# An attention and FFN block on one core: the probabilities of fifteen tiles transposed in 32x32 blocks on VectorE and put together through DRAM

## Chip, cores and metric

One Trainium2 chip, one of its cores. The metric is the device time of one execution of the whole program in microseconds. Three runs of the kernel before are known; their median is the number that the change is compared with. The profile comes from one further execution.

## What is computed

x has the shape 32 x 256 x 256 (batch, tokens, features), the context 32 x 77 x 256. One layer of cross-attention with a residual, then one gated FFN with a residual, all in fp32:

```
x = x + attention(layernorm(x), ctx)      8 heads of 32, 77 keys, causal mask, biases on q, k, v and out
h = silu(y @ w1.T * s1) * (y @ w2.T * s2)       y = layernorm(x), 256 -> 1024
h = gelu(h @ h1.T * h1s)                        1024 -> 1024
h = gelu(h @ h2.T * h2s)                        1024 -> 1024
x = x + h @ w3.T * s3                           1024 -> 256
attention:  p = softmax(mask(q @ k.T / sqrt(32)));  out = (p @ v) @ Wo.T + bo
```

The weights of the FFN are ternary, which one piece of a split fp32 number keeps exactly. So each of the FFN's products is made of two fast products (type fp32r), with the high and the low part of the activations. The attention's products are plain fp32.

## The kernel before

**Tiles and staging.** The 8192 tokens are 16 tiles of 512, each two batch entries (n = 0 and 1) of 256 tokens. All weights stay in SBUF. A prologue (FIRST, one_pass with f = None) does the attention of tile 0, computes the keys and values of all later tiles and spills them to DRAM. Then a loop runs whose pass f does the FFN of tile f, the attention of tile f + 1 and the load and first layernorm of tile f + 2. Two passes behind the loop finish the last tiles. So the attention of tile 0 is in the prologue and that of fifteen tiles in passes.

**The order.** ORDER (lines 57 to 66) is one list of steps written by hand. Each engine goes through it and issues what it has to do for each step; the engines meet through semaphores only. A step of the FFN is L1 n, L2 n, L3 n (n = 0 to 7, sixteen products of 128x512 for L2 and L3, eight for L1) or L4 n. The attention's steps stand between them: S (scores), MASK, MAX, SUB, EXP, SOFT (sum, reciprocal, product: the probabilities are finished), PT (transposes), PV (probabilities by values), O (output projection), LN2S and LN2A (second layernorm), T2 (its transpose), LN1S, ROWS, LN1A (first layernorm of the tile after), Q, and CTX (loads for the next tile). The attention uses four PSUM banks (ab), the FFN four others (fb).

**The steps that the change touches.** SOFT n leaves the probabilities of batch entry n in probs[:, 2n:2n+2, :], tokens on the partitions, for each token 8 heads of 77 keys (lines 906 to 912). The product with the values wants keys on the partitions. For that TensorE transposes in PT 0 to 3 (lines 598 to 613), one step for each 128 tokens, eight transposes each (L611), two steps for an entry; ScalarE copies four heads of a step from PSUM (L766) and VectorE the other four (L918) into attn_t for entry 0 and attn_t2 for entry 1, [77 keys, 8 heads, 256 tokens]. attn_t lies where L1's operand ln2_hi lies, attn_t2 where xln and out_sb lie, so the second copy waits until the output of the tile before is stored. PV n (lines 614 to 624) multiplies them with v_sb, both entries in a row; PV 0 waits for all copies. ScalarE copies the result to heads_t (L773), which O reads.

**Queues.** All transfers are issued by SyncE, in the order of the list: in CTX the keys (L361), the values (L362), and, when x1 is finished, x_in (L323) and ln_t (L326) of the tile after; in LN1S and ROWS two small transfers through DRAM (L331, L336); in L4 the output (L417). SyncE waits for each step's semaphore before it comes to the next.

**VectorE** also takes the low parts of the FFN's activations: L849 and L854 in L1, L860 in L2 and L3. TensorE needs those of L2 only at L3 0. A step of L2 n from 4 on needs ScalarE's evictions of step n - 4.

ln1_t, which holds the transposed x of the tile after, is used up to Q of the tile; k_t, the keys, up to S 1:

```
ln1_t, _ = put("ln1_t", [P, KD, TILE])
...
k_t, _ = put("k_t", [P, HG, NB * TK])
```

Of the kernel before, what the change touches and what calls it, by code (L numbers as in the profile page):

```python
# [16 lines left out]
F32 = mybir.dt.float32  # L17
# [6 lines left out]
P = 128  # L24
B, TQ, TK, D = 32, 256, 77, 256
H = 8
# [16 lines left out]
def column_of(head):  # L43
# [13 lines left out]
ORDER = [  # L57
    ("L1", 0), ("S", 0), ("MASK", 0), ("L1", 1), ("L1", 2), ("MAX", 0), ("S", 1), ("L1", 3), ("SUB", 0),
    ("L1", 4), ("L1", 5), ("L1", 6), ("L1", 7), ("L1E", 0),
    ("EXP", 0), ("MASK", 1), ("MAX", 1), ("SUB", 1), ("EXP", 1), ("SOFT", 0), ("L2", 0), ("SOFT", 1), ("L2", 1),  # L60
# [5 lines left out]
]  # L66
# [40 lines left out]
def build_kernel(nc, x, x_t, ctx_t, ctx_later, w_att, vectors, w1, w2, h1, h2, w3, out):  # L107
# [4 lines left out]
    with ExitStack() as es:  # L112
# [59 lines left out]
        out_sb, out_at = put("out_sb", [P, NQ, D])  # L172
        assert out_at == xln_at + 4 * NQ * D
        attn_t2, _ = put("attn_t2", [TK, H, TQ], at=xln_at)
        ln1_t, _ = put("ln1_t", [P, KD, TILE])
        x1_keep, _ = put("x1_keep", [P, NQ, D])
        ln1_rows, _ = put("ln1_rows", [P, 2, TILE], at=out_at)

        k_t, _ = put("k_t", [P, HG, NB * TK])
        v_sb, v_at = put("v_sb", [TK, NB, D])  # L180
        ctx_sb, _ = put("ctx_sb", [P, KD, NB * TK], at=v_at)


# [27 lines left out]
        flag, _ = put("flag", [1, 1], I32)  # L211

        rows_dram = nc.dram_tensor("ln1_rows_dram", (2, TILE), F32, kind="Internal").ap()
        k_dram = nc.dram_tensor("k_later_dram", (P, HG, LATER), F32, kind="Internal").ap()
        v_dram = nc.dram_tensor("v_later_dram", (LATER, D), F32, kind="Internal").ap()
        k_dram_tiles = k_dram.rearrange("p m (t c) -> t p m c", c=NB * TK)
# [36 lines left out]
        s_copied = sem("s_copied")  # L253
        sum_done, rsum_done, probs_ready = sem("sum_done"), sem("rsum_done"), sem("probs_ready")
        pt_ready, pt_act_done, pt_dve_done = sem("pt_ready"), sem("pt_act_done"), sem("pt_dve_done")
        pv_ready, heads_done, o_ready = sem("pv_ready"), sem("heads_done"), sem("o_ready")
        x_biased, x1_done, x1_kept = sem("x_biased"), sem("x1_done"), sem("x1_kept")
        t2_ready, ln2hi_done, ln2t_done = sem("t2_ready"), sem("ln2hi_done"), sem("ln2t_done")
# [62 lines left out]
        def _(sp):  # L321
# [51 lines left out]
            def one_pass(f, a, b, general):  # L373
                for step, n, t in steps(f, a, b):
                    if step in FFN and general:
                        for i, src in enumerate(general_chunks(step, n)):
                            c = chunk_base[step, n] + i
                            sp.wait_ge(ring_used, CHUNKS * f + c + 1)
                            sp.dma_start(ring[c % 2][:], src).then_inc(ring_loaded[c % 2], 16)
                    if step == "KEEP":  # L380
                        if n == 0:
                            for c in range(NP):
                                sp.wait_ge(piece_loaded[c], 16)
                        for c in KEPT[n]:
                            keep_piece(c)
                    if step == "SPILL" and n == 0:
                        sp.wait_ge(kx_done, 4)
                        spill_keys((0, 1), k_spilled[0])
                    if step == "SPILL" and n == 1:
                        sp.wait_ge(kx_done, 2 * NG - 1)  # L390
                        spill_keys(range(2, NG), k_spilled[1])
                        sp.wait_ge(vx_done, 5)
                        spill_values(range(0, 10))
                        sp.wait_ge(vx_done, (NCH + 1) // 2)
                        spill_values(range(10, NCH))
                    if step == "CTX":
                        sp.wait_ge(pv_ready, NB * t)
                        if f is None:
                            load_ctx(t)
                        else:  # L400
                            sp.wait_ge(k_spilled[0], 32)
                            sp.wait_ge(k_spilled[1], 16 * (NG - 2))
                            sp.wait_ge(v_spilled, 48)
                            load_keys_values(t, f)
                            sp.wait_ge(x1_done, t)
                            load_x(t)
                            load_xt(t)
                    if step == "LN1S" and f is not None:
                        write_rows(t)
                    if step == "ROWS":  # L410
                        sp.wait_ge(stored, 32 * f + 32)
                        load_rows(t)
                    if step == "L4":
                        half = slice(2 * n, 2 * n + 2)
                        sp.wait_ge(out_ready, 2 * f + n + 3)
                        dst = out_tiles[f] if isinstance(f, int) else out_tiles[bass.ds(f, 1)].rearrange("a p j d -> (a p) j d")
                        sp.dma_start(dst[:, half, :], out_sb[:, half, :]).then_inc(stored, 16)  # L417
# [29 lines left out]
        def _(pe):  # L447
# [35 lines left out]
            def one_pass(f, a, b, general):  # L483
                for step, n, t in steps(f, a, b):
# [113 lines left out]
                    if step == "PT":  # L598
                        if n % 2 == 0:
                            pe.wait_ge(probs_ready, NB * t + n // 2 + 1)  # L600
                        if n == 0:
                            pe.wait_ge(s_copied, NB * t + NB)
                            pe.wait_ge(masked, NB * t + NB)
                        if n == 1 and f is None:
                            pe.wait_ge(ln1t_done, 2)
                        if n == 2:
                            pe.wait_ge(pt_act_done, NQ * t + 2)
                            pe.wait_ge(pt_dve_done, NQ * t + 2)
                        pair = (2, 0, 2, 0)[n]
                        for h in range(H):  # L610
                            mm = nc.tensor.transpose(ab[0:TK, pair + h // 4, (h % 4) * P:(h % 4 + 1) * P],  # L611
                                                     probs[:, n, column_of(h) * TK:(column_of(h) + 1) * TK], id32[:])
                        mm.then_inc(pt_ready, 1)
                    if step == "PV":
                        if n == 0:
                            pe.wait_ge(pt_act_done, NQ * t + NQ)
                            pe.wait_ge(pt_dve_done, NQ * t + NQ)
                        bank = (2, 0)[n]
                        for g in range(HG):
                            for h in range(4):  # L620
                                mm = nc.tensor.matmul(ab[HD * h:HD * (h + 1), bank, g * TQ:(g + 1) * TQ],  # L621
                                                      v_sb[:, n, (4 * g + h) * HD:(4 * g + h + 1) * HD],
                                                      (attn_t, attn_t2)[n][:, 4 * g + h, :], start=True, stop=True)
                        mm.then_inc(pv_ready, 1)
                    if step == "O":
                        pe.wait_ge(heads_done, NB * t + NB)
# [61 lines left out]
        def _(act):  # L688
            def one_pass(f, a, b):
                for step, n, t in steps(f, a, b):  # L690
# [69 lines left out]
                    if step == "PT":  # L760
                        act.wait_ge(pt_ready, NQ * t + n + 1)
                        q0 = (n % 2) * P
                        pair = (2, 0, 2, 0)[n]
                        if n == 2 and f is not None:
                            act.wait_ge(stored, 32 * f + 32)
                        nc.scalar.copy((attn_t, attn_t2)[n // 2][:, 0:4, q0:q0 + P],  # L766
                                       ab[0:TK, pair, :].rearrange("p (h q) -> p h q", h=4)).then_inc(pt_act_done, 1)
                        if f is None and n < 2:
                            nc.scalar.copy(attn_t[:, 4:8, q0:q0 + P],
                                           ab[0:TK, pair + 1, :].rearrange("p (h q) -> p h q", h=4)).then_inc(pt_dve_done, 1)  # L770
                    if step == "PV":
# [14 lines left out]
        def _(dve):  # L786
# [42 lines left out]
            def one_pass(f, a, b):  # L829
                for step, n, t in steps(f, a, b):  # L830
# [75 lines left out]
                    if step == "SOFT":  # L906
# [3 lines left out]
                        nc.vector.reciprocal(per_head(rtotal, n), per_head(total, n)).then_inc(rsum_done, 1)  # L910
                        dve.wait_ge(rsum_done, NB * t + n + 1)
                        nc.vector.tensor_tensor(heads_of(n), heads_of(n), over_keys(rtotal, n), ALU.mult).then_inc(probs_ready, 1)
                    if step == "PT" and (f is not None or n >= 2):
                        dve.wait_ge(pt_ready, NQ * t + n + 1)
                        q0 = (n % 2) * P
                        if n == 2 and f is not None:
                            dve.wait_ge(stored, 32 * f + 32)
                        nc.vector.tensor_copy((attn_t, attn_t2)[n // 2][:, 4:8, q0:q0 + P],  # L918
                                              ab[0:TK, (2, 0, 2, 0)[n] + 1, :].rearrange("p (h q) -> p h q", h=4))\
                            .then_inc(pt_dve_done, 1)  # L920
# [144 lines left out]
```

## Time and profile before

| | |
|---|---|
| runs | 1598.69 us median of 3 (1598.31 to 1598.72) |
| profiled execution | 1598.01 us |
| its span, first to last instruction | 1596.2 us |
| granted TensorE clock, mean | 0.999 |
| TensorE busy | 1585.9 us, 8902 products |
| VectorE, ScalarE, GpSimd busy | 791.3, 728.5, 123.0 us |
| DMA | 67.73 MB, mean 42 GB/s |

The span leaves out what lies before the first and behind the last instruction, 1.8 us. Products on TensorE are pipelined: one begins before the last one ends, so the distance between the starts of two is what one costs in a row, and the duration of one is longer than that. In a timeline equal instructions that follow each other are merged into one row with their count; its second column is the time from the first one's start to the last one's end.

### The profile page before, as it was taken

The numbers are of one execution on the slowest core, as the hardware profiler recorded it, in microseconds if no ns is written. First come the engines' busy times: TensorE is split into PE (matmuls) and PEld (weight loads), VectorE is DVE, ScalarE is ACT, GpSimd is POOL, SyncE is SP. The second block draws the span as 40 slices with busy tenths as digits, with TensorE's granted clock in tenths as the row PEclk, the third lists the DMA queues.
The fourth block names the chain that finished last, engine by engine and source line by source line (L and its number), as shares of the span: only waits on it lengthen the run. The fifth ranks groups of instructions, "written<-read, shape, count | busy, mean of one in ns | idle before, by whom it ended". The sixth has DMA issues, their size and how long they took to land.

```text
span 1596.2 us, 22214 instructions
## 1 busy us (share of the span) xinstructions
PE 1585.9 (99%) x8902; PEld 1299.4 (81%) x8902; DVE 791.3 (50%) x1246; ACT 728.5 (46%) x1073; POOL 123.0 (8%) x134
## 2 busy tenths in 40 slices
PE   9999999999999999999999999999999999999998
PEld 6788888888888888888888888888888888888887
DVE  6653735447363464634537354464634537354332
ACT  4653534436353453534436354453634536354342
POOL 1001010010100101001010100101001010100000
PEclk9999999999999999999999999999999999999999
DMA  9921010100101001010000101001010010100000
GB/s 381 349 95 41 13 34 26 34 20 7 47 13 34 26 8 40 13 34 26 22 28 10 47 13 34 26 8 40 13 34 26 8 40 13 37 24 1 14 1 14
DMA packets 29349, 67.73 MB, mean 42 GB/s; under 512 B 6326, under 2 KB 14734, under 8 KB 26510
## 3 DMA queue, kind: packets, MB, share of 16 engines
q1 hardware_dynamic: 29326, 67.41, 11.8%
q8 instruction: 16, 0.26, 0.1%
q14 instruction: 7, 0.06, 0.0%
HBM read 43.00 MB, written 12.86 MB: 35 GB/s over the span
## 4 chain that ended last, share of the span: by engine, by line
PE 97%; DMA 1%; SPq 1%; DVE 0%; ACT 0%; issue 0%; ACTq 0%
PE ffn_banks L455 81%; PE att_banks L631 3%; PE att_banks L611 3%; PE att_banks L578 3%; PE att_banks L595 2%; PE att_banks L621 2%; DMA h_bits<-in_h 1%; PE att_banks L641 1%; SPq L365 0%; PE ffn_banks L664 0%; ACT junk L696 0%; SPq L344 0%; PE ffn_banks L656 0%; DVE inexact L834 0%; PE att_banks L566 0%
## 5 line engine op out<-in xcount | busy, mean ns | idle before, releaser
L455 PE MATMUL ffn_banks<-a_hi,h_sb 128*128 128x512 f32 x1024 | 405.8, 396 | 0.0
L455 PE MATMUL ffn_banks<-b_hi,h_sb 128*128 128x512 f32 x1024 | 399.7, 390 | 0.0
L455 PE MATMUL ffn_banks<-a_lo,h_sb 128*128 128x512 f32 x1024 | 399.0, 390 | 0.0
L455 PE MATMUL ffn_banks<-b_lo,h_sb 128*128 128x512 f32 x1024 | 398.5, 389 | 0.0
L860 DVE TENSOR_TENSOR b_lo<-b_f,b_hi 128x512 fp32r<-128x512 f32 x128 | 87.2, 691 | 288.2 <-ACT b_hi L731 288.2
L455 PEld LDWEIGHTS ffn_banks<-a_hi,h_sb 128*128 128x128 f32 x1024 | 192.3, 188 | 44.7 <-issue 6.2
L730 ACT ACTIVATE a_f<-ffn_banks,vec 128x512 f32<-128x512 f32 x128 | 88.3, 690 | 301.7 <-PE ffn_banks L455 301.7
L455 PEld LDWEIGHTS ffn_banks<-b_lo,h_sb 128*128 128x128 f32 x1024 | 192.3, 188 | 39.4
L455 PEld LDWEIGHTS ffn_banks<-b_hi,h_sb 128*128 128x128 f32 x1024 | 192.3, 188 | 39.4
L455 PEld LDWEIGHTS ffn_banks<-a_lo,h_sb 128*128 128x128 f32 x1024 | 192.4, 188 | 38.5
L860 DVE TENSOR_TENSOR a_lo<-a_f,a_hi 128x512 fp32r<-128x512 f32 x128 | 94.6, 739 | 258.4 <-ACT a_hi L731 258.4
L730 ACT ACTIVATE b_f<-ffn_banks,vec 128x512 f32<-128x512 f32 x128 | 88.1, 689 | 280.1 <-PE ffn_banks L455 278.7
L455 PE MATMUL ffn_banks<-ln_hi,w_sb 128*128 128x512 f32 x512 | 203.5, 398 | 0.6 <-DVE v_later L888 0.6
L455 PE MATMUL ffn_banks<-ln_lo,w_sb 128*128 128x512 f32 x512 | 200.4, 391 | 0.0
L714 ACT ACTIVATE a_f<-ffn_banks,vec 128x512 f32<-128x512 f32 x128 | 88.3, 690 | 163.1 <-PE ffn_banks L455 163.1
L455 PE MATMUL ffn_banks<-w_sb,a_hi 128*128 128x256 f32 x512 | 129.3, 294 | 0.8 <-DVE a_lo L860 0.8
L455 PE MATMUL ffn_banks<-w_sb,a_lo 128*128 128x256 f32 x512 | 123.6, 283 | 0.0
L849 DVE SCALAR_TENSOR_TENSOR a_f<-ffn_banks,vec,a_f 128x512 f32<-128x512 f32 x128 | 95.9, 749 | 52.9 <-PE ffn_banks L455 51.6
L455 PEld LDWEIGHTS ffn_banks<-ln_hi,w_sb 128*128 128x128 f32 x512 | 96.1, 188 | 22.7 <-issue 1.0
L455 PEld LDWEIGHTS ffn_banks<-ln_lo,w_sb 128*128 128x128 f32 x512 | 96.2, 188 | 19.4
L455 PEld LDWEIGHTS ffn_banks<-w_sb,a_hi 128*128 128x128 f32 x512 | 98.2, 192 | 4.7 <-issue 3.3
L455 PEld LDWEIGHTS ffn_banks<-w_sb,a_lo 128*128 128x128 f32 x512 | 98.2, 192 | 3.4 <-issue 3.3
(101 smaller groups left out, 1713.7 us busy)
## 6 DMA issues: line engine op xcount, KB each, us to landing
h_bits<-in_h SPq DMA_DIRECT2D x8, 1024.0 KB, 19.2
h_sb<-h_bits SPq DMA_DIRECT2D x8, 1024.0 KB, 8.4
out<-out_sb SPq DMA_DIRECT2D x32, 256.0 KB, 2.0
x_in<-in_x SPq DMA_DIRECT2D x15, 512.0 KB, 3.6
ln_t<-in_x_t SPq DMA_DIRECT2D x14, 512.0 KB, 4.3
ln_rows<-ln_rows_dram SPq DMA_DIRECT2D x14, 512.0 KB, 3.8
w_bits<-in_w SPq DMA_DIRECT2D x3, 1024.0 KB, 12.1
w_sb<-w_bits SPq DMA_DIRECT2D x3, 1024.0 KB, 6.6
```

The source lines that it names most:

```text
L455: mm = nc.tensor.matmul(psum, left, right, start=(k == 0 and part == 0), stop=(k == rows - 1 and part == 1))
L578: mm = nc.tensor.matmul(ab[:, m, :], wq_sb[:, k, m * P:(m + 1) * P], ln1_t[:, k, :], start=(k == 0), stop=(k == KD - 1))
L595: mm = nc.tensor.matmul(ab[:, h, at:at + TK], q_t[rows, g, tokens], k_t[rows, g, n * TK:(n + 1) * TK], start=True, stop=True)
L611: mm = nc.tensor.transpose(ab[0:TK, pair + h // 4, (h % 4) * P:(h % 4 + 1) * P], probs[:, n, column_of(h) * TK:(column_of(h) + 1) * TK], i ...
L621: mm = nc.tensor.matmul(ab[HD * h:HD * (h + 1), bank, g * TQ:(g + 1) * TQ], v_sb[:, n, (4 * g + h) * HD:(4 * g + h + 1) * HD], (attn_t, at ...
L631: mm = nc.tensor.matmul(ab[:, 2 + j // 2, (j % 2) * D:(j % 2 + 1) * D], heads_t[:, k, j * P:(j + 1) * P], wo_sb[:, k, :], start=(k == 0), ...
L641: mm = nc.tensor.transpose(ab[:, k, j * P:(j + 1) * P], xln[:, j, k * P:(k + 1) * P], id32[:])
L714: nc.scalar.activation(a_f32[:, n, :], fb[:, 2 * (n % 2), :], ACT.Silu, scale=s1_sb[:, n:n + 1]).then_inc(silu_done, 1)
L730: nc.scalar.activation(f32[:, n, :], fb[:, n % 4, :], ACT.Gelu, scale=scale[:, n:n + 1])
L849: nc.vector.scalar_tensor_tensor(out=a_f32[:, n, :], in0=fb[:, 2 * (n % 2) + 1, :], scalar=s2_sb[:, n:n + 1], in1=a_f32[:, n, :], op0=ALU. ...
L860: nc.vector.tensor_tensor(lo[:, n, :], f32[:, n, :], hi[:, n, :].bitcast(F32), ALU.subtract).then_inc(done, 1)
```

## The change

Only the tiles of the passes are changed; the prologue keeps PT. Each entry n has two new steps. DT n on VectorE: three block transposes of probs, each 32x32 block by itself, so that in the result keys lie on 32 partitions and tokens in runs of 32. Two take 32 keys of each of the 16 pairs of a head and a half of 128 tokens (blocks, 128 x 512 each), the third takes the last 16 keys (tail_blocks, 128 x 256). MV n on SyncE: stores blocks (512 KB) and tail_blocks (128 KB) to DRAM, waits for both, and issues four loads that put the four groups of 32 partitions side by side in attn_t or attn_t2: two of 32 partitions (256 KB each) and two of 13 partitions (52 KB each). PV n waits for the loads of its own entry and reads the tokens in runs of 32. blocks lies in ln1_t, tail_blocks in k_t; there is one of each, so DT 1 waits for the stores of MV 0. The list has PV behind L2 5 instead of L2 4, and O and CTX behind L2 7.

```diff
 ORDER = [
-    ("EXP", 0), ("MASK", 1), ("MAX", 1), ("SUB", 1), ("EXP", 1), ("SOFT", 0), ("L2", 0), ("SOFT", 1), ("L2", 1),
-    ("L2", 2), ("PT", 0), ("PT", 1), ("L2", 3), ("PT", 2), ("PT", 3), ("L2", 4), ("PV", 0), ("PV", 1),
-    ("L2", 5), ("L2", 6), ("O", 0), ("CTX", 0), ("L2", 7),
-    ("L3", 0), ("LN2S", 0), ("L3", 1), ("L3", 2), ("LN2A", 0), ("LN1S", 0), ("L3", 3), ("L3", 4), ("ROWS", 0),
+    ("EXP", 0), ("MASK", 1), ("MAX", 1), ("SUB", 1), ("EXP", 1), ("SOFT", 0), ("DT", 0), ("L2", 0), ("SOFT", 1), ("DT", 1),
+    ("L2", 1), ("MV", 0), ("L2", 2), ("MV", 1), ("L2", 3), ("L2", 4), ("L2", 5), ("PV", 0), ("PV", 1),
+    ("L2", 6), ("L2", 7), ("O", 0), ("CTX", 0), ("L3", 0), ("LN2S", 0), ("L3", 1), ("L3", 2), ("LN2A", 0), ("LN1S", 0), ("L3", 3), ("L3", 4), ("ROWS", 0),
...
+        blocks, _ = put("blocks", [P, 2, H * NB * 32], at=ln1_at)
+        tail_blocks, _ = put("tail_blocks", [P, H // 2 * NB * 32], at=k_at)
...
@@ SyncE
+                    if step == "MV":
+                        done = 2 * (NB * (t - 1) + n)
+                        sp.wait_ge(blocked, done + 1)
+                        sp.dma_start(blocks_dram[n], blocks[:]).then_inc(blocks_out, 16)
+                        sp.wait_ge(blocked, done + 2)
+                        sp.dma_start(tails_dram[n], tail_blocks[:]).then_inc(blocks_out, 16)
+                        if n == 0:
+                            sp.wait_ge(up_ready, KH * f + KH)
+                        else:
+                            sp.wait_ge(stored, 32 * f + 32)
+                        sp.wait_ge(blocks_out, 16 * done + 32)
+                        dst = (attn_t, attn_t2)[n][:].rearrange("k h q -> k (h q)").rearrange("k (r i) -> k r i", r=4)
+                        for c in range(2):
+                            src = blocks_dram[n][:, c, :].rearrange("(r k) i -> k r i", r=4)
+                            sp.dma_start(dst[32 * c:32 * c + 32], src).then_inc(blocks_back[n], 16)
+                        part = H * NB * 16
+                        for g in range(HG):
+                            src = tails_dram[n].rearrange("(r g k) i -> g k r i", r=4, g=HG)[g, 3:16]
+                            sp.dma_start(dst[64:TK, :, part * g:part * g + part], src).then_inc(blocks_back[n], 16)
@@ TensorE
                     if step == "PV":
-                        if n == 0:
-                            pe.wait_ge(pt_act_done, NQ * t + NQ)
-                            pe.wait_ge(pt_dve_done, NQ * t + NQ)
+                        if f is not None:
+                            pe.wait_ge(blocks_back[n], 64 * t)
+                        elif n == 0:
+                            pe.wait_ge(pt_act_done, NQ)
+                            pe.wait_ge(pt_dve_done, NQ)
                         bank = (2, 0)[n]
+                        by_block = (attn_t, attn_t2)[n][:].rearrange("k h q -> k (h q)")\
+                            .rearrange("k (r g j h q) -> k g h j r q", r=4, g=HG, j=NB, h=4)
                         for g in range(HG):
                             for h in range(4):
+                                probs_t = (attn_t, attn_t2)[n][:, 4 * g + h, :] if f is None else by_block[:, g, h]
@@ VectorE
+                    if step == "DT":
+                        dve.wait_ge(probs_ready, NB * t + n + 1)
+                        if n == 1:
+                            dve.wait_ge(blocks_out, 64 * t - 32)
+                        heads = probs[:, 2 * n:2 * n + 2, :].rearrange("p j (h g c) -> p g (j h) c", g=HG, c=TK)
+                        for c in range(2):
+                            op = nc.vector.transpose(blocks[:, c, :], heads[:, :, :, 32 * c:32 * c + 32])
+                        op.then_inc(blocked, 1)
+                        tails = probs[:, 2 * n:2 * n + 2, :].rearrange("p j (h c) -> p (j h) c", c=TK)[:, :, TK - 16:TK]
+                        nc.vector.transpose(tail_blocks[:], tails).then_inc(blocked, 1)
```

In the copies of PT on ScalarE and VectorE the conditions on f and the wait for `stored` fall away, since PT is left only in the prologue; `n == 1 and f is None` in TensorE's PT becomes `n == 1`.

## Rows read from the trace of the kernel before

**Rows 1.** The page, part 1: busy time, share of the span, instructions.
```profile
PE 1585.9 (99%) x8902; PEld 1299.4 (81%) x8902; DVE 791.3 (50%) x1246; ACT 728.5 (46%) x1073; POOL 123.0 (8%) x134
```

**Rows 2.** Busy times in one loop pass; last: granted clock, DMA share, GB/s.
```profile
738.26:834.57 96.31, 96.31 (x546) 79.17 (x545) 48.38 (x77) 44.00 (x65) 7.83 (x8) 1.00 0.08 25
```

**Rows 3.** The page, part 4: the chain that ended last, by engine and line.
```profile
PE ffn_banks L455 81%; PE att_banks L631 3%; PE att_banks L611 3%; PE att_banks L578 3%; PE att_banks L595 2%; PE att_banks L621 2%; DMA h_bits<-in_h 1%; PE att_banks L641 1%; SPq L365 0%; PE ffn_banks L664 0%; ACT junk L696 0%; SPq L344 0%; PE ffn_banks L656 0%; DVE inexact L834 0%; PE att_banks L566 0%
```

**Rows 4.** Waits of TensorE: in total, times, longest.
```profile
PE att_banks L611 <- DVE probs L912: 1.2, 1, 1.2
...
PE att_banks L621 <- DVE attn_t L918: 0.3, 1, 0.3
```

**Rows 5.** Timeline of TensorE, 757 to 800 us: start, length, instruction, count.
```profile
759.09 0.39 PE L455 MATMUL ffn_banks<-a_hi,h_sb 128*128 128x512 f32 x1
...
769.97 1.91 PE L611 MATMUL att_banks<-id,probs 128*77 128x128 f32 x16
771.63 0.48 PE L455 MATMUL ffn_banks<-a_hi,h_sb 128*128 128x512 f32 x1
...
775.36 1.91 PE L611 MATMUL att_banks<-id,probs 128*77 128x128 f32 x16
777.03 0.48 PE L455 MATMUL ffn_banks<-a_hi,h_sb 128*128 128x512 f32 x1
...
780.85 1.93 PE L621 MATMUL att_banks<-attn_t,v_sb 77*32 77x256 f32 x32
782.71 0.50 PE L455 MATMUL ffn_banks<-a_hi,h_sb 128*128 128x512 f32 x1
```

**Rows 6.** Groups of instructions by line and form: busy us, mean ns, idle before.
```profile
L611 PE MATMUL att_banks<-id,probs 128*77 128x128 f32 x512 | 61.1, 273 | 1.2 <-DVE probs L912 1.2
...
L918 DVE COPY attn_t<-att_banks 77x512 f32<-77x512 f32 x62 | 39.6, 679 | 0.0
...
L621 PE MATMUL att_banks<-attn_t,v_sb 77*32 77x256 f32 x512 | 30.9, 382 | 0.3 <-DVE attn_t L918 0.3
```

**Rows 7.** Timeline of VectorE in the same pass.
```profile
766.75 1.45 DVE L912 TENSOR_TENSOR probs<-probs,rtotal 128x1232 f32<-128x1232 f32 x1
768.96 0.69 DVE L860 TENSOR_TENSOR b_lo<-b_f,b_hi 128x512 fp32r<-128x512 f32 x1 [0.77 <-ACT b_hi L731]
769.57 1.43 DVE L908 TENSOR_REDUCE total<-probs 128x16 f32<-128x1232 f32 x1
...
771.32 1.44 DVE L912 TENSOR_TENSOR probs<-probs,rtotal 128x1232 f32<-128x1232 f32 x1
...
793.75 1.23 DVE L926 TENSOR_TENSOR x<-att_banks,x_in 128x1024 f32<-128x1024 f32 x1 [1.46 <-PE att_banks L631]
```

**Rows 8.** Timeline of SyncE's queue, 700 to 850 us: when it issued, for how long.
```profile
740.57 4.10 SPq L417 DMA_DIRECT2D out<-out_sb  x2
782.99 0.58 SPq L361 DMA_DIRECT2D k_t<-k_later_dram  x1
...
795.14 0.37 SPq L323 DMA_DIRECT2D x_in<-in_x  x1
795.60 0.38 SPq L326 DMA_DIRECT2D ln_t<-in_x_t  x1
```

**Rows 9.** DMA issues by transfer: count, size, median us from issue to landing.
```profile
out<-out_sb SPq DMA_DIRECT2D x32, 256.0 KB, 2.0
x_in<-in_x SPq DMA_DIRECT2D x15, 512.0 KB, 3.6
...
k_t<-k_later_dram SPq DMA_DIRECT2D x14, 154.0 KB, 2.7
...
k_later_dram<-k_later SPq DMA_DIRECT2D x4, 512.0 KB, 6.8
```

**Rows 10.** GB/s in 40 slices of 740:745 (out), then of 794:801 (x_in, ln_t).
```profile
GB/s 0 0 0 0 0 0 0 0 0 0 0 197 410 360 426 360 312 33 0 0 0 0 0 0 0 0 0 0 0 0 0 0 0 0 0 0 0 0 0 0
...
GB/s 0 0 0 0 0 0 0 0 0 0 0 0 117 164 94 351 328 328 374 234 257 421 421 375 398 421 374 398 445 281 211 0 0 0 0 0 0 0 0 0
```

More of the change, by code:

```diff
@@ L174, in build_kernel @@
         attn_t2, _ = put("attn_t2", [TK, H, TQ], at=xln_at)
-        ln1_t, _ = put("ln1_t", [P, KD, TILE])
+        ln1_t, ln1_at = put("ln1_t", [P, KD, TILE])
         x1_keep, _ = put("x1_keep", [P, NQ, D])
         ln1_rows, _ = put("ln1_rows", [P, 2, TILE], at=out_at)
-        k_t, _ = put("k_t", [P, HG, NB * TK])
+        k_t, k_at = put("k_t", [P, HG, NB * TK])
         v_sb, v_at = put("v_sb", [TK, NB, D])
+        blocks, _ = put("blocks", [P, 2, H * NB * 32], at=ln1_at)
+        tail_blocks, _ = put("tail_blocks", [P, H // 2 * NB * 32], at=k_at)
         ctx_sb, _ = put("ctx_sb", [P, KD, NB * TK], at=v_at)
@@ L213, in build_kernel @@
         rows_dram = nc.dram_tensor("ln1_rows_dram", (2, TILE), F32, kind="Internal").ap()
+        blocks_dram = [nc.dram_tensor(f"blocks_dram{n}", (P, 2, H * NB * 32), F32, kind="Internal").ap() for n in range(NB)]
+        tails_dram = [nc.dram_tensor(f"tails_dram{n}", (P, H // 2 * NB * 32), F32, kind="Internal").ap() for n in range(NB)]
         k_dram = nc.dram_tensor("k_later_dram", (P, HG, LATER), F32, kind="Internal").ap()
@@ L255, in build_kernel @@
         pt_ready, pt_act_done, pt_dve_done = sem("pt_ready"), sem("pt_act_done"), sem("pt_dve_done")
+        blocked, blocks_out = sem("blocked"), sem("blocks_out")
+        blocks_back = [sem("blocks_back0"), sem("blocks_back1")]
         pv_ready, heads_done, o_ready = sem("pv_ready"), sem("heads_done"), sem("o_ready")
@@ L603, in one_pass @@
                             pe.wait_ge(masked, NB * t + NB)
-                        if n == 1 and f is None:
+                        if n == 1:
                             pe.wait_ge(ln1t_done, 2)
@@ L614, in one_pass @@
                     if step == "PV":
-                        if n == 0:
-                            pe.wait_ge(pt_act_done, NQ * t + NQ)
-                            pe.wait_ge(pt_dve_done, NQ * t + NQ)
+                        if f is not None:
[3 more added lines that the diff above has]
+                            pe.wait_ge(pt_dve_done, NQ)
                         bank = (2, 0)[n]
+                        by_block = (attn_t, attn_t2)[n][:].rearrange("k h q -> k (h q)")\
+                            .rearrange("k (r g j h q) -> k g h j r q", r=4, g=HG, j=NB, h=4)
                         for g in range(HG):
                             for h in range(4):
+                                probs_t = (attn_t, attn_t2)[n][:, 4 * g + h, :] if f is None else by_block[:, g, h]
                                 mm = nc.tensor.matmul(ab[HD * h:HD * (h + 1), bank, g * TQ:(g + 1) * TQ],
                                                       v_sb[:, n, (4 * g + h) * HD:(4 * g + h + 1) * HD],
-                                                      (attn_t, attn_t2)[n][:, 4 * g + h, :], start=True, stop=True)
+                                                      probs_t, start=True, stop=True)
                         mm.then_inc(pv_ready, 1)
@@ L763, in one_pass @@
                         pair = (2, 0, 2, 0)[n]
-                        if n == 2 and f is not None:
-                            act.wait_ge(stored, 32 * f + 32)
                         nc.scalar.copy((attn_t, attn_t2)[n // 2][:, 0:4, q0:q0 + P],
                                        ab[0:TK, pair, :].rearrange("p (h q) -> p h q", h=4)).then_inc(pt_act_done, 1)
-                        if f is None and n < 2:
+                        if n < 2:
                             nc.scalar.copy(attn_t[:, 4:8, q0:q0 + P],
@@ L912, in one_pass @@
                         nc.vector.tensor_tensor(heads_of(n), heads_of(n), over_keys(rtotal, n), ALU.mult).then_inc(probs_ready, 1)
-                    if step == "PT" and (f is not None or n >= 2):
+                    if step == "DT":
+                        dve.wait_ge(probs_ready, NB * t + n + 1)
+                        if n == 1:
+                            dve.wait_ge(blocks_out, 64 * t - 32)
[5 more added lines that the diff above has]
+                        nc.vector.transpose(tail_blocks[:], tails).then_inc(blocked, 1)
+                    if step == "PT" and n >= 2:
                         dve.wait_ge(pt_ready, NQ * t + n + 1)
                         q0 = (n % 2) * P
-                        if n == 2 and f is not None:
-                            dve.wait_ge(stored, 32 * f + 32)
                         nc.vector.tensor_copy((attn_t, attn_t2)[n // 2][:, 4:8, q0:q0 + P],
```

## The prediction

> **What bounds the kernel now.** I read the busy line first: TensorE is busy for 1585.9 us of 1596.2, VectorE for half of the span [rows 1], and over one pass of the program's loop, 96.31 us, the granted clock is 1.00, its 2.4 GHz level [rows 2]. In the chain of waits the FFN's products (L455) hold 81% and the probabilities' transposes (L611) are 3% of the span [rows 3]. The table of TensorE's waits shows that it waits for nothing in the steady state: before L611 once, 1.2 us, before the product with the values (L621) once, 0.3 us [rows 4]. So an instruction taken off TensorE is worth its whole time, and every wait put on TensorE costs its whole time. 15 of the 16 tiles go through the changed steps; I follow one, from 759 to 783 us.
>
> **What is removed.** TensorE's timeline shows two blocks of 16 transposes in a tile [rows 5]. The first runs from 769.97 to 771.63, 1.66 us; the second from 775.36 to 777.03, 1.67 us. The L2 step behind the first lasts from 771.63 to 775.36, 3.73 us, where three undisturbed steps take 769.97 - 759.09 = 10.88, or 3.63 each: each switch to fp32 and back costs another 0.10. One tile gives 1.66 + 1.67 + 2 x 0.10 = 3.53 us, fifteen give **53.0 us**. (Mean durations of L611, 273 ns x 480 = 131 us, overlap and are no price [rows 6].) The evictions, a pair of copies for each transpose step on ScalarE and VectorE (679 ns on VectorE, L918 [rows 6]), go too; both engines have slack, so I count them at nothing.
>
> **What is added on VectorE.** A DT step is two block transposes of 128x512 and one of 128x256. No row has this operation. The nearest one is an SBUF-to-SBUF pass over 512 columns: L860 starts at 768.96 and the next independent instruction at 769.57, 0.61 us [rows 7]. I take 0.61 + 0.61 + 0.35 = 1.57 us for a step; half of it and twice of it are the bounds. The two steps cost VectorE 3.1 us a tile against 2.7 us of copies removed: its load stays at about half. What counts is their latency, in the next part.
>
> **What is added on the path: the way through DRAM.** In the new order TensorE runs L2 0 to L2 5 without a break: 759.09 + 6 x 3.63 = 780.87, and with the switch it starts PV 0 at 780.95 and wants PV 1 half a PV block later; that block is 1.86 us for both (780.85 to 782.71) [rows 5], so at **781.9**. Is the second half there?
> - SOFT 0 ends at 766.75 + 1.45 = 768.20 [rows 7]. DT 0 ends its big transposes at about 769.5 and its tail at 769.9. L860 comes behind it at 769.8 instead of 768.96, SOFT 1 starts at 770.4 instead of 769.57. It lasted 771.32 + 1.44 - 769.57 = 3.19 us, so it ends at 773.6.
> - DT 1 waits, on VectorE, for MV 0's two stores, since there is one buffer. SyncE issued a transfer 0.16 us after its cause (L926 ends 793.75 + 1.23 = 794.98 [rows 7], L323 at 795.14 [rows 8]). A store of 256 KB was issued at 740.57 [rows 8], had its first bytes 0.8 us later, moved for 0.75 us mostly at 360 to 420 GB/s and landed after 2.0 us [rows 9, 10]. The 512 + 128 KB are thus 0.8 + 1.75 + 0.45 = 3.0 us: 769.66 + 3.0 = 772.7, 0.9 us before VectorE gets there. No wait. If there were one, L860 of L2 1 and later stands behind it, which nobody needs before L3.
> - DT 1's second transpose ends at 773.6 + 1.25 = 774.85. SyncE has issued the four loads of MV 0 by then (772.8 to 775.1 at about 0.6 us each, below). MV 1's stores: 775.0 + 3.0, seen by SyncE at 778.1.
> - Four loads follow. Issuing k_t (three dimensions) took 0.58 us, x_in and ln_t came 0.46 us apart [rows 8]. I take 0.62, so that the fourth starts 1.85 us after the first, and for its landing that of k_t, 2.7 us for 154 KB [rows 9]. Together 4.55: **782.65**. The 616 KB themselves need 1.9 us at the 328 GB/s that x_in and ln_t together had in 3.2 us [rows 10], and are covered by that.
> - TensorE stands for 782.65 - 781.9 = 0.75 us, and I add 0.25 for being woken and refilling its pipeline: 1.0 us a tile, **15 us** in all.
>
> The bounds of the round trip: below, 2.0 + 3.6 us (one store of 256 KB, one load of 512 KB [rows 9], less than the data asks), which is before the need, no wait; above, 6.8 us for a store as under the load of the prologue [rows 9], which would add 3.8 and hold DT 1 back by 2.9 more, so up to 7.7 us a tile and 115 us. I take the value near the lower one, because the queue is empty around these steps as it was for the loop's transfers there.
>
> PV 0's half is early: its loads are issued at 772.8 and land by 777.4.
>
> Here a rule of the Trainium skill speaks against the change. Its page "SBUF — State Buffer" (Door 1: The DMA port swizzle) says that partitions 0 to 31 and 32 to 63 lie on the same eight of 16 ports, for an asymptote of 218 GB/s. The 512 KB of the two big loads would take 2.4 us by it instead of 1.6, and the sum would be about 1570. No row loads just 64 partitions, so the trace neither confirms nor denies it.
>
> **What else moves.** PV reads its moving operand in runs of 32 elements instead of 256. No row has such a read; between nothing (same columns, L621 379 ns [rows 6]) and twice 1.86 us a tile (28 us) I take nothing, the count of columns being unchanged. O moves behind L2 7. L3 0 then comes at once, where L2 7 used to lie between. The sum x1 (L926, 1.23 us and its latency [rows 7]) is ready some 1.6 us after O and its statistics are wanted on VectorE behind L3 0's eviction, so 3 us are in hand, and T2 is seven L3 steps away. SyncE's queue has MV ahead of CTX: k_t, v_sb, x_in and ln_t are issued up to one L2 step later; x_in lands 1.6 + 0.2 + 3.6 = 5.4 us after O's end [rows 9], and LN1S asks for it after three L3 steps, 10.9 us. The output stores are over 25 us before MV (740.57 [rows 8]), the row transfers behind it. All at nothing. The extra 2.5 MB a tile leave the DMA engines mostly idle.
>
> **Sum.** The profiled execution took 1598.01 us (span 1596.2), the median of the runs is 1598.69. 1598.0 - 53.0 + 15 = 1560.0; by the median **1561**.
>
> **Rivals.**
> - A, the forecast: a wait of 0.4 to 1.5 us before PV 1, 1551 to 1568 us. Chance 0.35.
> - B, no wait: the round trip is 6.9 us or less (stores at the 400 GB/s of the fastest slices, loads issued 0.46 us apart). Then 1598.7 - 53.0 = 1546, up to 1551. For it: x_in took 3.6 us for 512 KB. Against: four loads in line on one queue. Chance 0.22.
> - C, the loads into few partitions are slow: only half of the DMA engines' rate, some 200 GB/s (half of the 400 of the fastest slices [rows 10]), gets into 64 partitions. The 512 KB last 2.6 us, MV 1's stores stand behind MV 0's loads for 0.8 us, and the wait is 1.8 us: 1598.7 - 53.0 + 27 = 1573; with the DRAM side slower as well up to 3 us, 1591. Chance 0.29. It is the rule of the page named above, and its figure gives 1570.
> - D, slower than before: the block transposes take twice the 0.61 us. DT 0 shifts everything by 1.5 us and DT 1 by 1.25, TensorE waits 1.0 + 2.75 = 3.75 us in each tile: 1598.7 - 53.0 + 56 = 1602, and with C's 0.8 us on top 1614. It decides from a wait of 3.53 us a tile. Against it: the VectorE rows here take 1.2 ns a column whatever they compute (1.45 us for L912's 1232 columns, 0.61 for L860's 512 [rows 7]). Chance 0.11.
> - A wait between 3.3 and 3.7 us leaves the time within 0.2%, 0.03. That the change does nothing is excluded: L611 falls from 512 to 32.
>
> **Numbers.** 0.2% (3.2 us) is about what a measurement of this kernel can tell from no change. Faster: A, B and C, 0.86. Same 0.03. Slower 0.11. The range: B's end at 1544 to C's end at 1592.
>
> **What would show it.** L611 with 32 instructions; TensorE's waits with a new entry, L621 (PV) on a DMA into attn_t2, fifteen times about 1 us, and none on attn_t. VectorE's timeline: transposes of 0.6 us, SOFT 1 0.8 us later against L2's steps, no wait of DT 1. SyncE: stores landing 3 us after their issue, the fourth load some 7.8 us after DT 1's second transpose. The forecast is wrong if L621's instructions become longer, if the wait is at PV 0, or if a wait appears at S, T2, Q or L3 0.

## The result and the profile after

The changed kernel takes 1614.68 us (median of 4 runs, 1602.51 to 1625.65) against 1598.50 for the kernel before on the same chip: ratio 1.0102, 95% interval 1.007 to 1.0134. It is slower by 1.0%, where 1561 was forecast and 1592 was the end of the range. Its runs lie 23 us apart, those of the kernel before 1.4 us, and the time goes with the granted clock of the run: 1602.5 us at 0.988, 1614.3 at 0.979, 1615.0 at 0.980, 1625.7 at 0.973.

The page of the changed kernel, part 1 (busy us, share, instructions) and part 4 (the chain by engine), answering to [rows 1, 3]. Lines have moved: L479 is what L455 was, L650 (PV) was L621, L635 (PT) was L611, L887 was L860:

```profile
PE 1564.3 (97%) x8422; PEld 1263.2 (78%) x8422; DVE 800.6 (50%) x1276; ACT 697.2 (43%) x1013; POOL 123.0 (8%) x134
...
PE 73%; DVE 14%; DMA 8%; SPq 2%; issue 1%; ACT 1%; DVEq 0%; ACTq 0%
```

The transposes are gone (8902 - 8422 = 480 products), but TensorE no longer fills the span, and the chain that ends last now runs through VectorE and the DMA. Of TensorE's waits (total, times, longest) this one is new; in the kernel before no single wait was longer than 1.6 us, and none came back in every tile:

```profile
PE att_banks L650 <- DMA attn_t<-tails_dram: 37.7, 15, 3.2
```

Fifteen waits, one in each changed tile, 2.5 us on average, all at PV. TensorE's timeline around one of them (start, length, instruction, count, idle time before it), the place that [rows 5] show at 780.85:

```profile
785.75 0.39 PE L479 MATMUL ffn_banks<-a_lo,h_sb 128*128 128x512 f32 x1
786.07 1.07 PE L650 MATMUL att_banks<-attn_t,v_sb 77*32 77x256 f32 x16
789.38 1.49 PE L650 MATMUL att_banks<-attn_t,v_sb 77*32 77x256 f32 x16 [2.24 <-DMA attn_t<-tails_dram]
790.79 0.79 PE L479 MATMUL ffn_banks<-a_hi,h_sb 128*128 128x512 f32 x1
791.39 0.63 PE L479 MATMUL ffn_banks<-a_lo,h_sb 128*128 128x512 f32 x1
791.81 0.63 PE L479 MATMUL ffn_banks<-a_hi,h_sb 128*128 128x512 f32 x1
...
793.43 0.39 PE L479 MATMUL ffn_banks<-a_hi,h_sb 128*128 128x512 f32 x1
```

Two things stand here. PV 0 runs at once and as fast as before (16 instructions in 1.07 us; the row of 32 had 1.93), so the runs of 32 elements cost nothing. PV 1 begins 3.31 us after PV 0, where 0.93 would do, half of the 1.86 of [rows 5]; over the fifteen tiles it is 3.58 us on average. And behind the wait the FFN's products are 0.43 us apart instead of 0.23 and last 0.63 instead of 0.39, until about 793.1: TensorE goes on at half its rate. The windows view says why: its last three columns are the granted clock, the DMA share and GB/s. Four of the fifteen tiles, 10 us around PV:

```profile
105.00:115.00 10.00, 7.14 (x47) 4.15 (x46) 0.92 (x2) 2.33 (x4) 0.00 (x0) 0.78 0.31 76
397.00:407.00 10.00, 7.48 (x57) 5.05 (x56) 0.69 (x1) 2.39 (x5) 0.00 (x0) 1.00 0.40 95
587.00:597.00 10.00, 7.45 (x48) 4.43 (x47) 1.39 (x2) 2.33 (x5) 0.00 (x0) 0.75 0.32 74
785.00:795.00 10.00, 7.76 (x51) 4.87 (x50) 0.69 (x1) 2.33 (x4) 0.00 (x0) 0.83 0.38 95
```

In eleven tiles the clock falls to its 1.2 GHz level behind the wait (mean of the window 0.66 to 0.83), in four (one of them from 397) it does not. The length of the wait alone does not decide it: the four waited 2.3 to 2.5 us, the eleven 2.2 to 3.2. The mean over the span is 0.979 against 0.999: 0.020 x 1612 = 32 us of clock lost, a little of it in the idle time itself. The sum closes: 1598.7 - 53.0 (transposes) + 37.7 (waits) + 32 (clock) = 1615, the profiled execution took 1614.33.

SyncE's timeline of the same tile shows where the wait comes from (start, length, transfer):

```profile
774.68 0.34 SPq L404 DMA_DIRECT2D blocks_dram<-blocks  x1
775.13 0.37 SPq L406 DMA_DIRECT2D tails_dram<-tail_blocks  x1
777.69 0.80 SPq L415 DMA_DIRECT2D attn_t<-blocks_dram  x2
778.54 0.82 SPq L419 DMA_DIRECT2D attn_t<-tails_dram  x2
780.13 0.34 SPq L404 DMA_DIRECT2D blocks_dram<-blocks  x1
780.58 0.36 SPq L406 DMA_DIRECT2D tails_dram<-tail_blocks  x1
784.09 0.80 SPq L415 DMA_DIRECT2D attn_t<-blocks_dram  x2
784.93 0.82 SPq L419 DMA_DIRECT2D attn_t<-tails_dram  x2
```

This tile stands 5.13 us behind the one of the prediction (its L2 0 starts at 764.22 instead of 759.09). MV 0's first store was forecast for 769.66 + 5.13 = 774.79 and was issued at 774.68, MV 1's for 775.0 + 5.13 = 780.13 and was issued at 780.13. MV 0's stores took 3.01 us to the first load, as forecast. MV 1's took 3.96 (median of the fifteen tiles 4.10), and from the first of its loads to PV 1 it was 789.38 - 784.09 = 5.29 us instead of 4.55 + 0.25. The rates in those loads, GB/s in 40 slices of 784 to 790 us, where x_in and ln_t had 328 on average and up to 445 [rows 10]:

```profile
GB/s 0 0 0 0 0 0 0 150 68 218 259 382 410 396 301 219 232 218 218 212 198 205 205 157 103 55 0 0 0 0 0 0 0 0 0 0 0 0 0 0
```

After a peak of 410 GB/s the rate settles at about 200 to 230 GB/s.

### The profile page after: what moved, and what is told of

It reads as the page before. It is cut to its first block, busy times and chain, and to the rows that moved or that the text cites. A ratio compares the mean times of both kernels' runs of the same rounds, so it can differ in the third digit from the quotient of the medians.

```text
span 1612.4 us, 21318 instructions
## 1 busy us (share of the span) xinstructions
PE 1564.3 (97%) x8422; PEld 1263.2 (78%) x8422; DVE 800.6 (50%) x1276; ACT 697.2 (43%) x1013; POOL 123.0 (8%) x134
## 4 chain that ended last, share of the span: by engine, by line
PE 73%; DVE 14%; DMA 8%; SPq 2%; issue 1%; ACT 1%; DVEq 0%; ACTq 0%
PE ffn_banks L479 61%; DMA attn_t<-tails_dram 4%; DMA tails_dram<-tail_blocks 4%; PE att_banks L660 3%; PE att_banks L602 3%; DVE probs L939 3%; DVE total L935 2%; DVE blocks L946 2%; PE att_banks L619 2%; PE att_banks L650 2%; DVE mx L929 1%; DVE probs L932 1%; DMA h_bits<-in_h 1%; PE att_banks L670 1%; SPq L415 1%
## 5 line engine op out<-in xcount | busy, mean ns | idle before, releaser
L479 PE MATMUL ffn_banks<-a_hi,h_sb 128*128 128x512 f32 x1024 | 413.2, 403 | 0.0
L479 PE MATMUL ffn_banks<-a_lo,h_sb 128*128 128x512 f32 x1024 | 409.5, 400 | 0.0
L479 PE MATMUL ffn_banks<-b_hi,h_sb 128*128 128x512 f32 x1024 | 402.6, 393 | 0.0
L479 PE MATMUL ffn_banks<-b_lo,h_sb 128*128 128x512 f32 x1024 | 398.6, 389 | 0.0
L479 PEld LDWEIGHTS ffn_banks<-a_hi,h_sb 128*128 128x128 f32 x1024 | 199.9, 195 | 53.0 <-issue 10.5
L479 PEld LDWEIGHTS ffn_banks<-a_lo,h_sb 128*128 128x128 f32 x1024 | 199.8, 195 | 42.1
L887 DVE TENSOR_TENSOR a_lo<-a_f,a_hi 128x512 fp32r<-128x512 f32 x128 | 94.6, 739 | 269.0 <-ACT a_hi L760 269.0
L887 DVE TENSOR_TENSOR b_lo<-b_f,b_hi 128x512 fp32r<-128x512 f32 x128 | 84.6, 680 | 281.0 <-ACT b_hi L760 281.0
L479 PEld LDWEIGHTS ffn_banks<-b_hi,h_sb 128*128 128x128 f32 x1024 | 192.3, 188 | 39.4
L479 PEld LDWEIGHTS ffn_banks<-b_lo,h_sb 128*128 128x128 f32 x1024 | 192.3, 188 | 39.3
L479 PE MATMUL ffn_banks<-ln_hi,w_sb 128*128 128x512 f32 x512 | 203.6, 398 | 0.6 <-DVE v_later L915 0.6
L479 PE MATMUL ffn_banks<-ln_lo,w_sb 128*128 128x512 f32 x512 | 200.4, 391 | 0.0
L479 PE MATMUL ffn_banks<-w_sb,a_hi 128*128 128x256 f32 x512 | 129.3, 294 | 0.8 <-DVE a_lo L887 0.8
L479 PE MATMUL ffn_banks<-w_sb,a_lo 128*128 128x256 f32 x512 | 123.6, 283 | 0.0
L479 PEld LDWEIGHTS ffn_banks<-ln_hi,w_sb 128*128 128x128 f32 x512 | 96.1, 188 | 22.7 <-issue 1.0
L479 PEld LDWEIGHTS ffn_banks<-ln_lo,w_sb 128*128 128x128 f32 x512 | 96.2, 188 | 19.4
L479 PEld LDWEIGHTS ffn_banks<-w_sb,a_hi 128*128 128x128 f32 x512 | 98.2, 192 | 4.7 <-issue 3.4
L479 PEld LDWEIGHTS ffn_banks<-w_sb,a_lo 128*128 128x128 f32 x512 | 98.2, 192 | 3.4 <-issue 3.3
```

What stands on the lines that cost most here:

```text
L479: mm = nc.tensor.matmul(psum, left, right, start=(k == 0 and part == 0), stop=(k == rows - 1 and part == 1))
L887: nc.vector.tensor_tensor(lo[:, n, :], f32[:, n, :], hi[:, n, :].bitcast(F32), ALU.subtract).then_inc(done, 1)
```

## The experiments

Eight kernels were run beside the kernel before. The theory to be tested, **W**: the way through DRAM is 2.5 us late, and TensorE's idle time costs a second time, since the granted clock falls behind it. Rivals: **X**, the clock falls for another reason (transfers, strided reads); for the lateness **P**, the loads are slow because each reaches few partitions, against **L**, plain latency of many single transfers.

**e1: PV one L2 step later.**

```diff
...
-("L2", 5), ("PV", 0), ("PV", 1), ("L2", 6), ("L2", 7),
+("L2", 5), ("L2", 6), ("PV", 0), ("PV", 1), ("L2", 7),
...
```

> PV 0 and PV 1 stand one L2 step later (behind L2 6), nothing else is changed. Theory W (the loss is the wait before PV 1, 2.5 us a tile, and the fall of TensorE's granted clock that this idle time brings): the loads are there 1.2 us before the need, no wait, clock 0.998 or more, 1598.5 - 53 = 1545.5 us, between 1543 and 1550. Theory X (the clock falls because of the added transfers or of the strided reads of PV, whatever TensorE waits for): the wait goes, the clock stays at 0.98, 1565 to 1578 us.

Measured: 1546.17 us, ratio 0.9673 (0.9657 to 0.9689), runs from 1543.57 to 1546.66. The transfers are the same (store to load 3.01 and 4.14 us), the waits on DMA are gone, and the clock does not fall. The windows view, over 100 us:

```profile
700.00:800.00 100.00, 100.00 (x547) 81.44 (x546) 53.40 (x83) 45.06 (x66) 7.84 (x8) 1.00 0.16 50
```

TensorE's timeline, both PV steps in one row without a gap, as before:

```profile
759.82 1.93 PE L650 MATMUL att_banks<-attn_t,v_sb 77*32 77x256 f32 x32
```

So the transposes were worth 1598.6 - 1546.2 = 52.4 us, and 2.5 MB more a tile disturb nothing. X falls. This version beats both kernels.

**e2: the wait filled with work.**

```diff
+                        if f is not None and n == 1:
+                            for _ in range(10):
+                                nc.tensor.matmul(ab[:, 3, 0:P], id32[:], id32[:], start=True, stop=True)
```

> TensorE makes ten fp32 products of 128x128 by 128 columns into an unused bank between PV 0 and PV 1 of each tile (about 2.1 us by L660's pitch of 0.204 us for 256 columns), work of no use, in the time in which it stood. Theory W: the loads land as late as before, so the 37 us of the wait stay, but the clock stays up: 1598.5 - 53 + 15 x 2.5 = 1583 us, 1579 to 1589, clock 0.997 or more, and the spread of the runs is gone. Theory X: the clock falls all the same, 1610 to 1620 us.

Measured: 1587.18 us, 0.9928 (0.9912 to 0.9945), runs from 1586.79 to 1587.67, within 0.9 us. TensorE's timeline:

```profile
775.78 1.07 PE L653 MATMUL att_banks<-attn_t,v_sb 77*32 77x256 f32 x16
776.78 2.50 PE L641 MATMUL att_banks<-id 128*128 128x128 f32 x20
779.67 1.07 PE L653 MATMUL att_banks<-attn_t,v_sb 77*32 77x256 f32 x16 [0.39 <-DMA attn_t<-tails_dram]
```

PV 1 begins as late as in the changed kernel (on average 3.64 us after PV 0, there 3.58), TensorE does useless work instead of standing, and the kernel is 27.5 us faster for it, with the clock at 1.00 and the spread gone. That is the part of the clock, alone. The rest, 1587.2 - 1546.2 = 41.0 us, is the lateness: 2.7 us a tile.

**e7: half of that work.** The same edit with range(5).

> Five products of no use before PV 1 instead of ten: TensorE works for 1.05 us of the wait and stands for 1.4. Theory W: the loads land as before, so the time is that of e2 (1587) plus what the clock loses; with an idle stretch of 1.4 instead of 2.4 us the clock falls in fewer tiles or in none: 1585 to 1600 us, clock 0.99 or more.

Measured: 1590.75 us, 0.9955 (0.9939 to 0.9972), runs from 1587.63 to 1593.23. TensorE stands for 19.5 us in all, 1.3 in a tile; the clock (0.997) falls in two tiles of fifteen, the first and the last, where TensorE stood for 1.8 and 3.3 us; in the other thirteen it stood for 0.9 to 1.6 us. As expected.

**e5: PV one L2 step earlier**, behind L2 4.

```diff
...
-("L2", 4), ("L2", 5), ("PV", 0), ("PV", 1),
+("L2", 4), ("PV", 0), ("PV", 1), ("L2", 5),
...
```

> PV 0 and PV 1 stand one L2 step earlier (behind L2 4), so TensorE waits longer in every tile. Theory W: PV 0 now waits too, the waits of a tile sum to 2.5 + 3.63 = 6.1 us, 92 us in all; the clock falls in all 15 tiles, for 3.4 to 6.8 us each at 1.2 GHz, a loss of 26 to 51 us: 1546 + 92 + 26 to 51 = 1664 to 1689 us, clock 0.93 to 0.97. If the clock has another cause than TensorE's idle time, it stays at 0.98 and the time is 1546 + 92 + 30 = 1668, with the drops at the same 11 or so of the 15 tiles.

Measured: 1684.70 us, 1.054 (1.0523 to 1.0558). TensorE waits for 90.6 us, the clock (0.956) falls in all fifteen tiles. 138.5 us above e1: 90.6 of waits and some 48 of clock, near the upper end of what W gave; with another cause of the fall some eleven tiles were expected, not fifteen.

**e4: the order alone**, on the kernel before.

```diff
...
-("L2", 4), ("PV", 0), ("PV", 1), ("L2", 5), ("L2", 6), ("O", 0), ("CTX", 0), ("L2", 7),
+("L2", 4), ("L2", 5), ("PV", 0), ("PV", 1), ("L2", 6), ("L2", 7), ("O", 0), ("CTX", 0),
...
```

> The kernel before, transposes on TensorE, with the new places of PV (behind L2 5), O and CTX (behind L2 7). Both theories: nothing waits for these steps, 1598.5 us within 1.5 us, clock 0.999. If the order alone costs or gains, it shows here, as a wait at O, T2, Q or L3 0.

Measured: 1598.79 us, 1.0006 (0.9996 to 1.0016). The places of PV, O and CTX cost nothing by themselves.

**e3: the second load on other partitions.**

```diff
...
-                            sp.dma_start(dst[32 * c:32 * c + 32], src).then_inc(blocks_back[n], 16)
+                            at = (wide, wide2)[n][96 * c:96 * c + 32].rearrange("k h q -> k (h q)").rearrange("k (r i) -> k r i", r=4)
+                            sp.dma_start(at, src).then_inc(blocks_back[n], 16)
...
```

> The second of the two 256 KB loads goes to partitions 96 to 127 instead of 32 to 63: same bytes, pieces, issues and order. PV contracts over 32 keys only (its first product reads v_sb as moving operand), so the output lacks the other keys; the number of columns that TensorE streams is unchanged. Theory P (the loads are slow because both go into partitions 0 to 63): their data moves at about 400 GB/s instead of 210, MV 1's stores land 3.1 us after their issue instead of 3.9, the last load about 4.2 us after the first issue instead of 5.2, the wait falls from 2.4 us to 0.4 to 1.0, 1550 to 1562 us. Theory L (the round trip is latency and the queue of single transfers): stores 3.9, loads 5.2, wait 2.4, 1602 to 1625 us as in the changed kernel.

Measured: 1640.95 us, 1.027 (1.0253 to 1.0287). Both of P's numbers failed: the stores took 4.10 us again (median), and PV 1 began 804.08 - 798.51 = 5.57 us after the first load's issue. That looked like L, though the time lies above L's range too. But the design has a hole: the loads go through one queue in order, so the second may well move only behind the first (argued, not shown), and each reaches 32 partitions wherever these lie. And TensorE's part was not left as it was:

```profile
800.40 0.62 PE L655 MATMUL att_banks<-v_sb 77*32 77x256 f32 x2
800.95 1.06 PE L655 MATMUL att_banks<-attn_t,v_sb 32*32 32x256 f32 x14
804.08 1.06 PE L655 MATMUL att_banks<-v_sb 77*32 77x256 f32 x2 [2.07 <-DMA attn_t<-tails_dram]
805.07 1.92 PE L655 MATMUL att_banks<-attn_t,v_sb 32*32 32x256 f32 x14
```

A PV now takes 1.6 us instead of 1.07, and the clock fell in all fifteen tiles (0.969), though TensorE stood for 32.7 us only, less than in the changed kernel. The run decides nothing about P.

**e6: each load over all 128 partitions.**

```diff
...
-                            src = blocks_dram[n][:, c, :].rearrange("(r k) i -> k r i", r=4)
-                            sp.dma_start(dst[32 * c:32 * c + 32], src).then_inc(blocks_back[n], 16)
+                            sp.dma_start(dst[:, 512 * c:512 * c + 512], blocks_dram[n][:, c, :]).then_inc(blocks_back[n], 16)
...
```

> The two 256 KB loads go to all 128 partitions, 2 KB to each (same bytes, same number of 2 KB pieces, same issues); PV multiplies what lies in the first 1024 columns, so the output is not the attention's, with the same products as before. Putting the second load on other partitions changed nothing, as each load by itself still reached only 32 partitions. Theory P' (what counts is how many partitions one load reaches): MV 1's first load is issued 3.1 to 3.3 us after its store instead of 4.1, PV 1 can start 4.2 us after it instead of 5.3, the wait falls from 2.4 to under 0.6 us, and the clock stays up: 1546 to 1556 us. Theory L (latency and single file): 4.1 and 5.3 us, 1602 to 1625.

Measured: 1558.84 us, 0.977 (0.975 to 0.9791). PV and the tails' loads are changed as said there. SyncE's timeline of one tile:

```profile
756.45 0.34 SPq L406 DMA_DIRECT2D blocks_dram<-blocks  x1
...
759.64 0.80 SPq L416 DMA_DIRECT2D attn_t<-blocks_dram  x2
```

TensorE's timeline:

```profile
762.39 1.07 PE L651 MATMUL att_banks<-attn_t,v_sb 77*32 77x256 f32 x16
763.97 1.07 PE L651 MATMUL att_banks<-attn_t,v_sb 77*32 77x256 f32 x16 [0.51 <-DMA attn_t<-tails_dram]
```

GB/s in 40 slices of 759 to 765 us:

```profile
GB/s 109 41 0 0 0 0 0 0 0 0 82 82 164 218 273 328 314 355 423 437 348 287 314 225 144 103 62 48 0 0 0 0 0 0 0 0 0 0 0 0
```

Store to load 3.19 us (median 3.11), load to PV 1 4.33 (median 4.45, in the changed kernel 5.29), rates up to 437 GB/s, wait 0.7 us a tile (10.2 in all), clock 1.00. The same bytes in the same number of pieces and issues: L falls. The lateness beyond the forecast comes from the few partitions that a load reaches, and it enters twice, in MV 1's stores and in its loads. By what path it does so is shown in part only. The row of rates counts a piece where it begins, and summed up it holds 631 KB in 2.70 us here and in 2.85 us in the changed kernel's row. Over the fifteen tiles the last piece ends 3.73 us after the first load's issue (median; 4.38 in the changed kernel), and the last of the loads' semaphore updates comes at 4.41 us (5.25 there). So 0.65 of the 0.84 us are in moving the pieces and the rest in their landing. The time is 2.8 us above what was expected. The profiled execution, 1556.94 us, is where the wait of 0.7 us puts it (1546.2 + 10.2); two of the other three runs had a clock of 0.998 and 0.996, so here too it fell at times.

**e9: MV 0's loads behind MV 1's stores.** In MV 0 only the stores are left; MV 1 issues its stores, then the four loads of entry 0, then its own.

```diff
...
+                        for m in range(NB if n == 1 else 0):
+                            if m == 0:
+                                sp.wait_ge(up_ready, KH * f + KH)
+                            else:
+                                sp.wait_ge(stored, 32 * f + 32)
+                                sp.wait_ge(blocks_out, 16 * done + 32)
...
```

> MV 0's four loads are issued behind MV 1's stores instead of ahead of them; MV 1's loads follow. Theory Q (MV 1's stores are late, 4.1 us instead of 3.0, because MV 0's loads are ahead of them in the queue): now both stores take 3.0 us, PV 0's data come later (about 6 us after MV 1's store, just in time), MV 1's loads are issued 1.1 us earlier but have MV 0's loads ahead of them, so the wait becomes 1.5 to 2.5 us: 1575 to 1615 us. If stores of MV 1 still take 4.1 us, something else than the loads holds them.

Measured: 1638.13 us, 1.0253 (1.0236 to 1.027). SyncE's timeline, MV 1's store and its own first load (the third row):

```profile
794.72 0.32 SPq L404 DMA_DIRECT2D blocks_dram<-blocks  x1
...
795.64 1.21 SPq L416 DMA_DIRECT2D attn_t<-blocks_dram  x2
...
797.94 0.78 SPq L416 DMA_DIRECT2D attn_t<-blocks_dram  x2
```

The stores take at most 3.22 us instead of 4.10: SyncE issues its own loads then without having waited for them. So Q holds, the loads ahead of the stores had held them up. The remedy is worse than the ill. PV 0's data were expected just in time; now PV 0 waits for 1.0 to 1.9 us as well, TensorE stands for 53.5 us in all in thirty waits, the clock falls in every tile (0.968), and the time is above the 1615 at which the expected range ended.

TensorE's waits for the loads in e2, e7, e6, e3, e9 and e5 (total, times, longest):

```profile
PE att_banks L653 <- DMA attn_t<-tails_dram: 2.2, 6, 0.7
...
PE att_banks L653 <- DMA attn_t<-tails_dram: 19.5, 15, 3.3
...
PE att_banks L651 <- DMA attn_t<-tails_dram: 10.2, 15, 1.5
...
PE att_banks L655 <- DMA attn_t<-tails_dram: 32.7, 15, 2.8
...
PE att_banks L651 <- DMA attn_t<-tails_dram: 53.5, 30, 2.3
...
PE att_banks L650 <- DMA attn_t<-tails_dram: 90.6, 30, 6.2
```

All runs beside each other (idle: TensorE's waits for the loads in the profiled execution; the tiles with a fall are counted there too, by the granted clock):

| | idle us a tile | tiles with a fall | mean clock | time us |
|---|---|---|---|---|
| e1 | 0 | 0 | 1.00 | 1546.2 |
| e6 | 0.7 | 0 | 1.00 | 1558.8 |
| e2 | 0.15 | 0 | 1.00 | 1587.2 |
| e7 | 1.3 | 2 | 0.997 | 1590.8 |
| changed kernel | 2.5 | 11 | 0.979 | 1614.7 |
| e9 | 3.6 in two | 15 | 0.968 | 1638.1 |
| e3 | 2.2, slow PV | 15 | 0.969 | 1641.0 |
| e5 | 6.0 | 15 | 0.956 | 1684.7 |

## Why the prediction was wrong

**What held.** The value of the transposes: 53.0 us forecast, 52.4 by e1. VectorE's steps: in its timeline two block transposes of 512 columns take 1.30 us from the first one's start to the last one's end and the last one itself 0.69, so they start 0.61 apart, as taken; rival D falls. That D's second figure, 1614, is the measured time is a coincidence: it was made of slow transposes, which did not come, and without the clock.

```profile
773.35 1.30 DVE L946 STREAM_TRANSPOSE blocks<-probs 128x512 f32<-128x512 f32 x2
774.58 0.40 DVE L949 STREAM_TRANSPOSE tail_blocks<-probs 128x256 f32<-128x256 f32 x1
```

The timeline up to MV 1's store, within 0.11 us. No wait of DT 1 worth naming. The strided reads of PV and the new places of O and CTX at nothing (e1, e4). Without the wait the time would have been rival B's 1546.

**The term that was mis-sized: the wait before PV 1, "1.0 us a tile", 15 us in all.** TensorE stands for 2.5 us a tile, and PV 1 is 2.7 us late (it begins 3.58 us after PV 0 on average, in e1 0.89; e2 has the same 2.7). Two entries of that sum were too small, by one mechanism. "MV 1's stores: 775.0 + 3.0": they take 4.1, since MV 0's loads are ahead of them (e9). "Together 4.55" for the loads to land: 5.25 (median). The 0.25 added for waking and refilling had no row behind it; from the last of the loads' semaphore updates to PV 1 it is 0.04 us (median). The forecast took the 616 KB at the 328 GB/s of [rows 10] as covered by the latency; the loads that reach 32 partitions settle at 200 to 230, those over 128 reach 437 and land 0.84 us sooner (e6). This is rival C's mechanism, with a wait of 1.8 to 3.0 us foreseen for it, and it was given 0.29. The Trainium skill's page "SBUF — State Buffer" (Door 1: The DMA port swizzle) has this rule, and the trace is near its 218 GB/s; that it is the ports which set the rate, no run here shows by itself. The same page says under "Can I just issue two DMAs to hit both halves?" that they serialize; e3 agrees so far as its PV 1 came no sooner (5.57 us after the first load's issue). The forecast should have gone by C for the wait. C's own times, 1573 to 1591, would have missed as well, by the next term.

**The term that was missing.** A wait was priced at its own length ("every wait put on TensorE costs its whole time"). With the right wait the sum would have been 1546 + 40 = 1586, inside the range and still faster. The kernel before had no place in its loop at which TensorE stood, so its trace could not show what idle time does to the clock: it showed 1.00 in the pass [rows 2], and the prediction took that as given. Measured, a wait of 2.5 us a tile costs 1614.7 - 1587.2 = 27.5 us more, and this part turned a gain of 0.7% into a loss of 1.0%. It also explains the spread: the wait is nearly the same in each tile (2.2 to 3.2 us), but the clock falls in some tiles and not in others, for a shorter or a longer time, and the runs' times follow their granted clocks (0.988 to 0.973). The Trainium skill's page "TensorE: Matmul & The Clock Gate" (Part 1) has the mechanism, that idle TensorE is put back to 1.2 GHz; the trace agrees with its two levels (products 0.43 us apart behind the wait, 0.23 before it).

**Left open.** What exactly, beside the length of the wait, decides whether the clock falls: in the changed kernel a wait of 2.5 us did not bring it down in one tile and one of 2.2 did in another; e3 stood for less time than the changed kernel and fell in all tiles, and differs in that its products used 32 rows and came slower, which was not tried alone. Whether the DRAM side adds to the 200 to 230 GB/s was not tried either, and e6 does not tell the ports from anything else that goes with a load's partitions, such as the bytes that each of them takes (8 KB against 2 KB in a load).

## To carry to other kernels

Where one engine is busy all the time, moving work off it to a long way round pays in full, but only if the consumer is placed behind the latest time at which the data land: here one step of 3.63 us later turned +1.0% into -3.3%. Price idle time of TensorE not at its length alone but with what the clock takes behind it, above all in a kernel whose trace has never shown a gap. And size a load by the partitions that it reaches: the same bytes landed after 5.25 us over 32 partitions at a time and after 4.41 over 128, and the stores next in the same queue paid 1.0 us for it too.

## What was not expected of the hardware

- Useless products in a wait made a kernel faster: e2 does 300 instructions more on TensorE than the changed kernel (busy 1572.1 against 1564.3 us) and takes 27.5 us less.
- The clock stayed low for longer than the wait that brought it down: in the tile shown TensorE stood for 2.24 us, and ran at half rate up to 793.1, 3.7 us behind the wait's end; in e5, behind PV 1's wait of 5.7 us, the granted clock has a mean of 0.68 over 12 us:

```profile
823.00:835.00 12.00, 10.97 (x46) 7.93 (x47) 0.69 (x1) 1.85 (x3) 0.00 (x0) 0.68 0.10 26
```
- A block transpose of 128x512 in fp32 on VectorE takes 0.69 us (median of 60), the same as a subtraction of that size (L887, 0.68 to 0.69).
